# A two-layer graph network on one core: message sums split between the two groups of the next pair, and their addition moved to the next step

## The reference

```python
# layer 0
m   = silu(concat(h[src], h[dst], ef) @ W1 + b1) @ W2 + b2
agg = segment_sum(m, dst)
h0  = silu(concat(h, agg) @ W3 + b3) @ W4 + b4 + h
x   = layernorm(x + h0)
# layer 1
z   = (1 + eps) * h + segment_sum(h[src], dst)
r   = relu(z @ V1 + c1) @ V2 + c2 + h
x   = layernorm(x + relu(layernorm(r) * gamma + beta))
```

## Time and profile before

| What | Value |
|---|---|
| median of 3 runs | 1939.5 us |
| lowest and highest run | 1931.52 and 1940.32 us |
| span of the profiled execution | 1500.6 us |
| the profiled execution's own time | not given |
| mean granted TensorE clock | 0.945 |

### The profile page before, as it was taken

One profiled execution on the slowest core, in us unless ns is written; L12 is line 12 of the kernel. 1 busy time (PEld: TensorE's weight loads), 2 busy tenths in 40 slices (PEclk: granted clock), 3 DMA queues, 4 the chain that ended last, 5 costly groups with the idle time before them and its releaser, 6 DMA issues.

```text
span 1500.6 us, 31339 instructions
## 1 busy us (share of the span) xinstructions
PE 1285.9 (86%) x8165; PEld 1063.6 (71%) x8165; DVE 1014.5 (68%) x2310; ACT 642.1 (43%) x1257; POOL 1107.0 (74%) x1164
## 2 busy tenths in 40 slices
PE   6788789778777889888888888885999999999992
PEld 6666667556556667767767776764899999998982
DVE  4678888677665565665566656643666888878866
ACT  2744556555555555555556555551111111111111
POOL 5777777777777777777777777777777777777771
PEclk9898889999998999999999999997999999999996
DMA  6533333333336454454455445433887778778731
GB/s 206 135 85 92 93 95 94 95 96 91 95 90 119 118 138 125 126 136 131 125 131 133 125 128 135 113 80 105 258 261 230 208 230 241 222 230 241 213 92 47
DMA packets 189124, 214.15 MB, mean 143 GB/s; under 512 B 60426, under 2 KB 149517, under 8 KB 189011
## 3 DMA queue, kind: packets, MB, share of 16 engines
q1 hardware_dynamic: 138399, 131.62, 28.9%
q0 software_dynamic: 36352, 74.52, 21.3%
q10 hardware_dynamic: 14260, 6.68, 1.6%
HBM read 202.74 MB, written 9.85 MB: 142 GB/s over the span
## 4 chain that ended last, share of the span: by engine, by line
POOL 42%; PE 32%; issue 15%; DVE 4%; DMA 4%; SPq 1%; ACT 1%; DVEq 0%; ACTq 0%; POOLq 0%
POOL gath L873 42%; PE bank L1434 9%; PE bank L1410 8%; PE bank L1362 4%; DMA gath<-src_term,src_col 2%; PE bank L1240 2%; PE bank L1250 2%; PE bank L1233 2%; PE bank L1421 1%; DMA T<-in_x 1%; DMA gath<-layer_input,src_col 1%; PE bank L1396 1%; PE bank L1383 1%; PE bank L1441 0%; PE bank L1456 0%
## 5 line engine op out<-in xcount | busy, mean ns | idle before, releaser
L873 POOL DMA_INDIRECT gath<-src_term,src_col x768 | 737.2, 960 | 234.2 <-issue 230.2
L873 POOL DMA_INDIRECT gath<-layer_input,src_col x336 | 329.6, 981 | 105.6 <-issue 100.6
L1240 PE MATMUL bank<-gath,ident 128*128 128x512 f32 x384 | 218.3, 652 | 114.5 <-DMA gath<-src_term,src_col 113.8
L1233 PEld LDWEIGHTS bank<-terms_r,terms_l 128*128 128x128 f32 x1568 | 209.4, 201 | 83.1 <-issue 69.2
L1233 PE MATMUL bank<-terms_r,terms_l 128*128 128x128 f32 x1568 | 219.6, 286 | 30.4 <-ACT msg L1022 22.0
L1923 DVE TENSOR_SCALAR_CACHE_REDUCE terms_l<-dst_bc,node_col 64x512 f32<-64x512 int32 x196 | 221.0, 1128 | 13.1 <-issue 7.2
L1250 PEld LDWEIGHTS bank<-oh,msg 128*128 128x128 f32 x1568 | 198.7, 202 | 26.9 <-issue 26.1
L1934 DVE TENSOR_TENSOR S<-S,bank 128x128 f32 x98 | 28.1, 286 | 270.2 <-PE bank L1252 178.2
L1250 PE MATMUL bank<-oh,msg 128*128 128x128 f32 x1568 | 202.3, 285 | 0.0
L1434 PE MATMUL bank<-S 128*128 128x288 f32 x672 | 170.0, 406 | 0.1
L1649 DVE TENSOR_TENSOR oh<-bank,dst_rel 128x1024 f32<-128x1024 f32 x140 | 169.8, 1213 | 0.0
(11 more groups left out here) (219 smaller groups left out, 1754.7 us busy)
## 6 DMA issues: line engine op xcount, KB each, us to landing
dst_bc<-in_dst SPq DMA_DIRECT2D x195, 128.0 KB
xT<-sorted_src SPq DMA_DIRECT2D x42, 512.0 KB
xs<-layer_input SPq DMA_DIRECT2D x136, 128.0 KB
gath<-src_term,src_col POOLq DMA_INDIRECT x768
terms_l<-layer_input SPq DMA_DIRECT2D x88, 128.0 KB
terms_r<-layer_input SPq DMA_DIRECT2D x88, 128.0 KB
msg<-layer_input SPq DMA_DIRECT2D x80, 128.0 KB
ef_s<-in_edge_attr SPq DMA_DIRECT2D x97, 64.0 KB
```

Of the source, the lines that this page charges most:

```text
L873: g.indirect_dma_start(out=to[:, j * D:(j + 1) * D], out_offset=None, in_=table[0:rows, :], in_offset=bass.IndirectOffsetOnAxis(ap=indices ...
L1233: mm(bank[h][:, j * D:(j + 1) * D], terms_l[:, u, h, j, :], terms_r[:, u, h, j, :], start=j == 0, stop=False)
L1240: mm(bank[h][:, :], ident[:, :], gath[:, slot, :], start=False, stop=True).then_inc(pre_ps, 1)
```

## The change

`pre_sums` and `message_sums` become functions of the group h of a pair, and TensorE's list names them alternately: first group's values of pair s-2, first half of the message sums of pair s-3, second group's values, second half. The first half carries the waits for `oh_made` and `sums_added`, the second half the degree product and the signal. `pre_sums` waits for `ohT_made` of its own group instead of the pair's second. On VectorE `add_sums` gets lag 4 and stands at the head of the list. Step `SORTED + 1` gets a wait for `oh_made`, since it overwrites the PSUM area that `one_hots` reads.

```diff
-            def pre_sums(k, m, q):
-
-                u = m % 2
-                pe.wait_ge(efT_made, done(k))
-                pe.wait_ge(ohT_made, done(2 * k + 1))
-                for h in range(2):
+            def pre_sums(h):
+                def body(k, m, q):
+
+                    u = m % 2
                     g = 2 * k + h
+                    pe.wait_ge(efT_made, done(k))
+                    pe.wait_ge(ohT_made, done(g))
                     pe.wait_ge(msg_made, done(g - 2))
...
-            def message_sums(k, m, q):
-                u = m % 2
-
-                pe.wait_ge(oh_made, done(k))
-                pe.wait_ge(sums_added, done(k - 2))
-                for c in range(2 * CH):
-                    if c % CH == 0:
-                        pe.wait_ge(msg_made, done(2 * k + c // CH))
-                    mm(bank[2 + u][:, 0:PW], msg[:, 2 * u + c // CH, c % CH * D:(c % CH + 1) * D], oh[:, u, c, :],
-                       start=c == 0, stop=c == 2 * CH - 1)
-                mm(bank[2 + u][0:1, PW:2 * PW], deg_col[:, m:m + 1], ident[:, :],
-                   start=True, stop=True).then_inc(sums_ps, 1)
+            def message_sums(h):
+                def body(k, m, q):
+                    u = m % 2
+
+                    if h == 0:
+                        pe.wait_ge(oh_made, done(k))
+                        pe.wait_ge(sums_added, done(k - 2))
+                    pe.wait_ge(msg_made, done(2 * k + h))
+                    for j in range(CH):
+                        mm(bank[2 + u][:, 0:PW], msg[:, 2 * u + h, j * D:(j + 1) * D], oh[:, u, h * CH + j, :],
+                           start=h == 0 and j == 0, stop=h == 1 and j == CH - 1)
+                    if h == 1:
+                        mm(bank[2 + u][0:1, PW:2 * PW], deg_col[:, m:m + 1], ident[:, :],
+                           start=True, stop=True).then_inc(sums_ps, 1)
+                return body
...
-                  of_early(3, early_kept), of_pair(1, turn_ef), of_pair(2, pre_sums), of_early(3, early_sums),
+                  of_early(3, early_kept), of_pair(1, turn_ef), of_pair(2, pre_sums(0)), of_early(3, early_sums),
                   of_early(2, early_rows), (0, NPAIR, keys_taken),
-                  of_unit_in(FIRST_BEFORE, UNITS - 1, 9, hnew_read), of_pair(3, message_sums),
+                  of_unit_in(FIRST_BEFORE, UNITS - 1, 9, hnew_read), of_pair(3, message_sums(0)),
+                  of_pair(2, pre_sums(1)), of_pair(3, message_sums(1)),
...
                 elif s == SORTED + 1:
+                    dve.wait_ge(oh_made, done(s - 2))
...
-                5: weight_products, **{k + 2: lambda k=k: keep_from_x(k) for k in range(FROM_X)}}), *in_banks(9, rows0),
-                  of_early(4, add_early), of_pair(1, windows), of_pair(2, one_hots(0, sums_ps, oh_made)),
-                  of_unit(9, ordered_norm0), of_pair(3, add_sums), (0, NPAIR, sort_edges),
+                5: weight_products, **{k + 2: lambda k=k: keep_from_x(k) for k in range(FROM_X)}}), of_pair(4, add_sums),
+                  *in_banks(9, rows0), of_early(4, add_early), of_pair(1, windows), of_pair(2, one_hots(0, sums_ps, oh_made)),
+                  of_unit(9, ordered_norm0), (0, NPAIR, sort_edges),
```

More of the change, by code:

```diff
@@ L1236, in pre_sums @@
                         add_from_x(g, bank[h])
-                        continue
+                        return
                     slot = 2 * m + h
```

## The result

The changed kernel is faster: 1871.4 us (median of 4 runs, 1870.5 to 1876.6) against 1937.2 us (4 runs) for the kernel before. The ratio is 0.969, 95% interval 0.966 to 0.972, a gain of 65.7 us. Forecast was no change.

What follows compares the result with a forecast made beforehand. The prediction took GpSimd's issuing of gathers to bound the edge stage, with every term 0 on the end and ±4.6 us for the port: 1939.5 + 0 = 1939.5 us, range 1927 to 1951 us.

Steps and rivals of the forecast that it cites:

- The 438.9 us: Difference between the profiled span, 1500.6 us, and the runs' median, 1939.5 us; taken to enter both kernels alike.
- It was lag inside the ring: on the end 0: VectorE's idle time before the addition, 100 to 240 us: up to 11.1 us of lag may go, 0 on the end.
- the wait for gathers: TensorE's waiting for the second group's gather, said to absorb the 0.98 us of half sums moved ahead of that group.
- TensorE's reordered products: Edge stage on TensorE: eight message records, 0.98 us, now stand between a pair's two groups; 0 on the end.
- the waits carried along: TensorE's first half waits earlier for the one-hot tile: 1.21 us per pair where VectorE is late, elsewhere 0.
- the port: VectorE's work moved against GpSimd's gathers: 0 on the end, within 4.6 us either way.
- the drain: End of the edge stage near 1034.7 us: compute leg about 1.7 us shorter but already 2.5 us early; 0.
- The rule that the prediction sets beside the port: A VectorE instruction in two-port mode keeps GpSimd from writing descriptors, so gathers under the moved sorting copies would be stretched.
- The faster rival: The early stretch's pace counts: 11.1 us off, 1928.4 us; at most 96 us with waits gone at every pair; chance 0.11.
- the later sums: VectorE's sum comes later by one step's sorting; TensorE's node update may wait, but would have waited for the windows anyway.
- The slower rival: Gather slots run dry in the sorting stretch: 30.7 us lag against 19.3 in hand, GpSimd stops 11.4 us, 1950.9 us; chance 0.09.

Runs made afterwards that it cites:

- the halves: TensorE's new order without VectorE's move, and VectorE's move without TensorE's order, each against the kernel before on a quick chip: 1.0002 and 1.000.
- the change with extra work: Changed kernel with the first half of each pair's message sums run twice, against the kernel before on a quick chip: 0.999 (0.9985 to 1.0004).
- few gathers: Three of four gathers per group left out in layer 0 from group 12; quick chip: kernel before 1368.4 us, changed kernel 1410.3 us, against 1499.9 us for the unedited kernel before.

## Why the prediction was wrong

**The pace of the profile was taken for the pace of the timed runs.** This is the step that failed: "They enter both kernels alike as far as anything here shows, so I work out a difference on the span and add it to the median." The 438.9 us did not lie around the span. The timed executions were 29% slower inside it. There GpSimd's queue, which "shows no gap over 0.3 us" in the profile, stops once or twice in every pair. So the terms that were put at nothing because "It was lag inside the ring: on the end 0", or because the cover was "the wait for gathers", had no such cover: at the slow pace GpSimd is idle for 495.8 us ahead of the 768 gathers in the kernel before and for 441.4 us in the changed kernel on the same chip, where the sum had no difference. The prediction named the possibility ("in a timed execution another engine might set the pace") and gave the rival that rests on it 0.11. A median 29% above the profiled span should have counted for more: it said by itself that the argument from the span covers at most 1500 of 1940 us.

**On the profile that was read, the forecast held.** At the quick pace the halves gave 1.0002 and 1.000, and the change with extra work 0.999; the gathers of a pair still take 10.1 us. TensorE's reordered products, the waits carried along, the port (gathers of 955 to 960 ns on the mean in every run, has 960) and the drain cost nothing on the end, as worked out. The rule that the prediction sets beside the port is hardly tested by these times, though: the sorting's copies at L1736 write the PSUM area `bank`, and are not copies within SBUF.

**One part of the change was left out.** The prediction has only eight message records change their place. The second group also moves behind the early products for layer 1, up to twelve records from 612 us on, and all of layer 0's gain at the slow pace arises behind 654 us.

**The faster rival came true, by another mechanism and at another size.** It was priced at 11.1 us, or up to 96 us with a gain in every pair, and argued away with "whatever makes an execution longer must also be kept off the gathers". It is not kept off them: at the slow pace the other engines' waits end late behind the gathers, and GpSimd then stops for lack of free slots. Measured were 65.7 us. The gain is not the VectorE idle time of that price. It goes along with two short stops of GpSimd for one long one: 12.4 instead of 13.4 us a pair from 600 us on.

**VectorE's move was mis-signed in the sorting stretch.** I wrote that "up to 11.1 us of the lag behind the gathers may go". With the move alone, group 36 was done at 235.96 us and GpSimd reused its slot at 246.53: 10.6 us in hand, against 22.5 us in the kernel before and 23.6 us with TensorE's order alone, all at the quick pace. The two rows, of TensorE and of GpSimd:

```profile
234.05 1.91 PE L1240 MATMUL bank<-gath,ident 128*128 128x512 f32 x2
...
246.53 1.00 POOL L873 DMA_INDIRECT gath<-src_term,src_col  x1 [0.30 <-issue]
```

The sentence on the later sums, "the next step's windows would have made TensorE wait there as well", is where that went wrong: the wait of the node update for the sums (1.89 us above) is new.

**The slower rival was half right.** The ring does get drained in the sorting stretch, by 12 us, but by VectorE's move and not by the one-hots and half sums that I priced at 30.7 us. It never reached GpSimd. With few gathers, when there is no such cover, the whole change costs 41.9 us. The Trainium skill's rule that I set beside this rival (TensorE: Matmul & The Clock Gate, engine queue depths; queues strictly in order) agrees with the trace: VectorE runs nothing in the 1.67 us ahead of the addition.

**Left open.** Why an execution has the slow pace, and whether it is the chip at all. Whether the gathers' issue or the bytes they move holds the releases back. Which of the products between the two groups make the runs of four; a run with the second group behind the early products and the message sums left at the end would tell. That the shorter runs of gathers cause the gain is argued from the timelines and the sum; no run forced runs of four on the old order. The changed kernel itself was never timed at the quick pace; its halves and the variant with extra work stand for it. VectorE's 0.4% at the slow pace has not been traced to a place: from 600 to 1000 us its pace is that of the kernel before (13.42 and 13.38 us a pair).

## What to carry to other kernels

Compare the span of a profile with the timed runs before anything else; here an execution's own time is its span plus 1.9 us. If they differ by more than some microseconds, the profile may be of another pace, and a bound read from it (here: a queue without a gap) need not hold in the timed runs. Where releases come late while one engine issues a long run of transfers, try to spread what frees its slots, so that it stops often and briefly; here that went along with 3%. Write down everything that a new order moves, not only what the change is named after. And a neutral change can hide a loss: here one of 42 us lies behind the gathers at the quick pace, and would appear if they became shorter.

## What was unexpected of the hardware

The same single-core program runs at 1500 or about 1900 us, with GpSimd's and VectorE's instructions of the same length (a gather 955 to 960 ns on the mean, the one-hot tile 1.21 us). Their part of the difference is idle time alone. TensorE is busy for 1471 us instead of 1286 in the kernel before, at a mean granted clock of 0.864 instead of 0.945, and idle for longer too. At the slow pace, waits that should end with another engine's signal end some 2 us after a run of gathers (4.45 and 4.82 us of idle on ScalarE and VectorE above), and TensorE stops for 1.0 to 1.2 us between products that wait for nothing. From 240 to 1000 us the kernel before has 34 such stops of over 0.5 us between two products of one line at the slow pace, and none at the quick one. With a quarter of the gathers such waits of VectorE, ScalarE and GpSimd are gone from 240 to 600 us at the slow pace and come to six from 600 to 1000 us, where the kernel before has 77; the gap between the paces shrinks from 395 us (1894.5 against 1499.9) to 185 us (1553.3 with TensorE's order against 1368.4 in the old order), of which 105 lie in the second layer (535 against 430 us).
